# Batches 2 to 4 of an adapter and cross-attention kernel: ranks and logits by columns from standing weights and split x

## What is computed

```python
# first layer, on x
logits = einsum('bsh,nh->bsn', x, router_W) + router_b   # 8 experts
w = softmax(logits)
a_sum = einsum('bsh,arh->bsr', x, ctx)                   # 64 ranks, summed over the 4 context batches
y = einsum('bsr,nhr->bsnh', a_sum, lora_B)
out = nan_to_num(x + 0.5 * einsum('bsn,bsnh->bsh', w, y))
# second layer: cross-attention of out to ctx, 32 heads of 32, masked softmax,
# output projection, residual, layer norm with gain and shift
```

## Time and profile before

| what | value |
|---|---|
| median of 3 runs | 643.59 us (643.53 to 644.02) |
| the profiled execution | 643.8 us, its span 641.9 us |
| busy share PE / DVE / ACT / POOL | 98 / 78 / 53 / 42% |
| mean granted TensorE clock | 0.994 of full |
| DMA | 114.14 MB, 53.4% of the engines' time |

### The profile page before, as it was taken

One profiled execution on the slowest core, in us unless ns is written; L12 is line 12 of the kernel. 1 busy time (PEld: TensorE's weight loads), 2 busy tenths in 40 slices (PEclk: granted clock), 3 DMA queues, 4 the chain that ended last, 5 costly groups with the idle time before them and its releaser, 6 DMA issues.

```text
span 641.9 us, 10730 instructions
## 1 busy us (share of the span) xinstructions
PE 629.0 (98%) x3455; PEld 544.9 (85%) x3455; DVE 500.7 (78%) x907; ACT 337.7 (53%) x1000; POOL 268.0 (42%) x357
## 2 busy tenths in 40 slices
PE   8999999999999999999999999999999999999993
PEld 8988889888988889888888888888888888888883
DVE  5689995578457774677468899999999999999635
ACT  6454463123242242322268778787777787777520
POOL 0020001000020002000335556888888998888874
PEclk9999999999999999999999999999999999999997
DMA  8936685436774467722857993425354344522312
GB/s 299 410 128 177 178 306 179 156 82 210 233 264 149 114 235 240 280 80 68 258 151 261 383 376 96 132 99 181 82 165 150 117 148 120 174 85 84 114 50 99
DMA packets 103399, 114.14 MB, mean 178 GB/s; under 512 B 57008, under 2 KB 76080, under 8 KB 103344
## 3 DMA queue, kind: packets, MB, share of 16 engines
q1 hardware_dynamic: 103152, 113.20, 53.4%
q10 hardware_dynamic: 192, 0.26, 0.2%
HBM read 67.29 MB, written 46.14 MB: 177 GB/s over the span
## 4 chain that ended last, share of the span: by engine, by line
PE 95%; DVE 2%; DMA 1%; issue 1%; ACT 0%; DVEq 0%; SPq 0%; POOL 0%; POOLq 0%; ACTq 0%
PE ps L602 26%; PE ps L603 26%; PE ps L604 26%; PE ps L664 4%; PE ps L747 4%; PE ps L760 2%; PE ps L761 2%; PE ps L635 1%; PE ps L638 1%; PE ps L636 1%; PE ps L674 1%; DMA stage<-WkT 1%; DVE u_lo L885 0%; DVE cx_sum L981 0%; DVEq L209 0%
## 5 line engine op out<-in xcount | busy, mean ns | idle before, releaser
L1258 POOL TENSOR_TENSOR u_sb<-a_sb,w_sb 128x512 f32<-128x512 f32 x16 | 19.6, 1245 | 236.2 <-DVE w_sb L879 231.3
L602 PE MATMUL ps<-wo_hi,cx_hi 128*128 128x512 f32 (+1 forms) x264 | 105.9, 401 | 0.0
L1185 ACT ACTIVATE s_sb<-s_sb,s_min 128x64 f32<-128x64 f32 x256 | 85.8, 338 | 34.6 <-DVE s_min L959 34.6
L604 PE MATMUL ps<-wo_hi,cx_lo 128*128 128x512 f32 (+1 forms) x264 | 101.7, 385 | 0.0
L603 PE MATMUL ps<-wo_lo,cx_hi 128*128 128x512 f32 (+1 forms) x264 | 101.6, 385 | 0.0
L602 PE MATMUL ps<-act_hi,w_hi 128*128 128x512 f32 x256 | 100.9, 394 | 0.3 <-DVE q_sb L933 0.3
L603 PE MATMUL ps<-act_lo,w_hi 128*128 128x512 f32 x256 | 99.8, 390 | 0.0
L604 PE MATMUL ps<-act_hi,w_lo 128*128 128x512 f32 x256 | 99.8, 390 | 0.0
L1150 ACT ACTIVATE act_hi<-h_t 128x512 fp32r<-128x512 f32 x32 | 20.3, 633 | 111.8 <-DVE h_t L922 111.8
L981 DVE SCALAR_TENSOR_TENSOR cx_sum<-ps,bias_c,cx_raw 64x256 f32<-64x256 f32 x128 | 61.8, 483 | 8.8 <-ACT cx_raw L1199 4.8
L1269 POOL TENSOR_TENSOR s_sb<-s_sb,s_inv 128x512 f32<-128x512 f32 x64 | 67.0, 1047 | 0.0
(11 more groups left out here) (119 smaller groups left out, 1543.1 us busy)
## 6 DMA issues: line engine op xcount, KB each, us to landing
q_cols<-q_sb SPq DMA_DIRECT2D x32, 512.0 KB, 3.6
qb<-q_cols SPq DMA_DIRECT2D x64, 256.0 KB, 4.0
x_sb<-xT SPq DMA_DIRECT2D x32, 256.0 KB, 3.2
h_rows<-hn_sb SPq DMA_DIRECT2D x64, 128.0 KB, 3.0
output_weights<-wo_sb SPq DMA_DIRECT2D x32, 256.0 KB, 2.5
z_sb<-h_rows SPq DMA_DIRECT2D x16, 512.0 KB, 4.7
out<-z_sb SPq DMA_DIRECT2D x15, 512.0 KB, 2.9
stage<-WvT SPq DMA_DIRECT2D x8, 512.0 KB, 4.6
```

Source lines behind the costliest of these rows:

```text
L602: pe.matmul(dst, lh, rh, start=(first and j == 0), stop=False)
L604: mm = pe.matmul(dst, ll, rh, start=False, stop=(last and j == n - 1))
L1185: act.activation(s_sb[c % 4][:, h, :], s_sb[c % 4][:, h, :], ACT.Exp, bias=s_min[c % 2][:, h:h + 1], scale=-1.0, accum_out=s_sum[c % 2][:, ...
```

## The change

Batch 1 keeps its routing. For the other three:

- **Ranks by columns** (`tokens` on PE, `x_parts` on the others). x is split like every other operand: ACT copies x_hi, POOL (even chunks) or DVE (odd) subtracts x_lo, in three buffers. The adapter's weights stand: two stationary 128-column tiles per chunk, a_w[0] and a_w[1], made once by POOL in a new stage `adapter`; three matmuls of 512 columns per chunk give ps_a, with 64 ranks and 8 logits in rows. The low part of the adapter for ranks is placed in the columns that would be free, and DVE adds the two.
- **Softmax and spread** (`spread`, `weigh`): ACT copies ps_a to a_t, DVE transposes 32x32 blocks so that the logits of a token lie in one partition, does the softmax there (Exp on ACT), splits the weights into high and low, writes them in four blocks and transposes back; ACT copies w_rows.
- **Growing u** (`grow`): four matmuls with `choose` (ones in chosen rows, made once on POOL) as stationary operand spread two experts' weights each over 128 rows; DVE multiplies each by a_t (u_f), ACT copies u_hi, DVE subtracts u_lo. The pass over POOL and the transposes on PE are gone.
- **Places in the list**: chunks are split from the first query step on, used after the second, third and fourth (a step later each for batch 2); the spread behind the fourth, `weigh` behind the sixth, `grow` behind the seventh. For batch 2 one step later, and `grow` stands behind the first half's `leave`. Of the keys, parts 2 and 3 go behind the fifth and sixth step, k_hi of parts 2 and 3 share the buffers of 0 and 1 and wait for stores, the mask's load goes behind the first step. x's loads count on four semaphores, not one.

The core of the diff:

```diff
+            beside[i][0] += parts(i + 1, 0, 1, 2)
+            beside[i][1] += tokens(i + 1, 0, 1, 2) + parts(i + 1, 3, 4, 5)
+            beside[i][2] += tokens(i + 1, 3, 4, 5) + parts(i + 1, 6, 7)
+            beside[i][3] += tokens(i + 1, 6, 7) + [("spread", i + 1)]
+            beside[i][5] += [("weigh", i + 1)]
+            beside[i][6] += [("grow", i + 1)]
-            beside[i][3] += [("route", i + 1)]
-            beside[i][5] += [("expand", i + 1, 0)]
-            beside[i][6] += [("expand", i + 1, 1)]
...
+            def tokens(i, k):                                    # PE
...
+                pe.wait_ge(xlo_even if low_on_pool(k) else xlo_odd, n + 1)
+                pe.matmul(ps_a, a_w[0][:, k, :], x_h, start=(k == 0), stop=False)
+                pe.matmul(ps_a, a_w[0][:, k, :], x_l, start=False, stop=False)
+                pe.matmul(ps_a, a_w[1][:, k, :], x_h, start=False, stop=(k == KC - 1)).then_inc(a_mm, 1)
+            def grow(i):                                         # PE
...
+                pe.wait_ge(route_act, 3 * i + 1)
+                pe.wait_ge(t_ready, KC * i)
+                for j in range(RC):
+                    rows = slice(B * j, B * j + 4)
+                    pe.matmul(ps_w[j], choose[rows, :], w_rows[rows, :], start=True, stop=True).then_inc(w_mm, 1)
...
+            def x_parts(i, k):                                   # ACT
+                act.wait_ge(x_in[k // 2], 32 * (i + 1))
+                act.wait_ge(up_mm, KC * i)
+                if k >= 3:
+                    act.wait_ge(a_mm, KC * (i - 1) + k - 2)
+                act.activation(x_hi[k % 3][:], x_sb[:, k, :], ACT.Copy).then_inc(xhi_done, 1)
...
             def key_parts(b):                                    # ACT
                 if b == 0:
                     act.wait_ge(k_copied, KC)
-                if b == NB - 1:
-                    act.wait_ge(mask_step, 4)
+                if b >= 2:
+                    act.wait_ge(k_stored, 32 * b)
...
+            def grow(i):                                         # DVE
+                def low(j):
+                    dve.wait_ge(uhi_done, RC * i + j + 1)
+                    dve.tensor_tensor(u_lo[:, j, :], u_f[j % 2][:], u_hi[:, j, :], ALU.subtract).then_inc(ulo_done, 1)
+                for j in range(RC):
+                    if j >= 2:
+                        low(j - 2)
+                        dve.wait_ge(ulo_done, RC * i + j - 1)
+                    dve.wait_ge(w_mm, RC * (i - 1) + (j + 1 if j < 2 else RC))
+                    dve.tensor_tensor(u_f[j % 2][:], ps_w[j], a_t[:], ALU.mult).then_inc(u_made, 1)
+                low(2)
+                low(3)
```

246 lines of the change are left out of this document (179 added, 67 removed).

## The result

| | before | after |
|---|---|---|
| median (lowest to highest) | 643.79 us (643.53 to 644.02), 4 runs | 686.77 us (686.08 to 688.07), 4 runs |
| ratio, 95% interval | | 1.0668 [1.0654, 1.0681] |
| profiled execution, its span | 643.8, 641.9 | 686.1, 684.3 |

The direction and the chains that PE waits for held; the size did not, the clock's above all.

The account below looks back on a forecast made before the run. PE's in-order matmul stream was taken as the bound. Batches 2, 3 and 4 (+10.0, +8.3, +7.8, saved columns included) and the clock (+4) gave +30 on 643.8, less 0.2 for the median: 674 us, range 660 to 684.

Parts of the forecast that it names:

- Columns: PE's matmul work in batches 2 to 4: fewer columns streamed, -2.5 us per batch, -7.6 us in all.
- a) First x chunk: Before each batch's first token matmul, PE waits for x_hi behind act_hi, then POOL: 5.3, 3.7, 3.2 us.
- Rival 3: All waits are covered and only columns count, if x_hi leaves ACT before PE arrives: 636 us, chance 0.06.
- b) The spread: DVE's dependent chain after the last token matmul takes 5.5 us, bounds 4.5 and 9.
- rival 2: The spread is long, its links taking up to 0.6 us: +3.5 us per batch, 684 us, chance 0.13.
- c) Batch 2's keys: Late key stores and shared k_hi buffers stall PE 3.3 us at the weights, 4.0 us at the next query step.
- d) Split 5: Batches 3 and 4: output-weight split 5's load, released by split 3 behind the spread, delays u_f; 7.5 us stall each.
- e) The clock: PE's granted clock falls in two stalls surely, perhaps half the others: 4 us in all, bounds 0 and 18.
- f) Start: POOL's new work before 25 us may slow DVE's splits there: taken as nothing, bound +1.5 us.
- Rival 1: The output-weight load of split 5 is in time or the spread short, query stalls 3.6 us: 664 us, chance 0.17.

Follow-up runs that it names:

- e10_order: The change reordered only: batches 3 and 4 with later tokens and first update, output-weight splits before the spread, grow behind exits; batch 2 also reordered; 657.1 us.
- e4: The change with key part 2 split ahead of batch 2's spread instead of behind it, nothing else; 684.4 us.
- e6: The change with batches 3 and 4's new work one query step earlier, plus batch 2's x splits and key parts 2 and 3 earlier; 668.3 us.
- e1: The change with the output-weight split of query step 3 put ahead of the spread, nothing else; 677.3 us.
- e12_gaps: The kernel before, with idle gaps made by hand on PE ahead of second-half query step 4 in batches 1 to 3; 655.5 us.
- e13: e10_order with x splits 3 to 5 directly behind the first tokens, and weigh, grow and last output-weight split later in batches 3 and 4; 666.1 us.
- e7: The e1 kernel with grow of batches 3 and 4 moved behind the first half's exits; 678.7 us.

## Why the prediction was too low

Against the profiled execution it said +30, and +42.3 came.

- **Columns** (-7.6): the balance closes with this term within a microsecond (rest 11.2 against 10.6 us counted at the slow pitch; 5.2 against 5.2 in e10_order). Its part on the four weights' matmuls was wrong: that 4 rows would "neither cost nor save" fails, since the four run together, and my estimate of the saving is now 8.4 (7.6 and 0.8).
- **a) First x chunk**: 5.3, 3.7, 3.2 forecast; 5.20, 3.56, 3.06 measured. Right, in size too, though the later chunks were called in time and one was late by 0.53. (Rival 3 mixes starts and ends of x_hi: by its ends ACT stands 3.9, 2.3 and 1.8 us behind.)
- **b) The spread**: 5.5 forecast; in batch 3 from DVE's first link at 195.60 to its last at 200.86 plus 0.71, 6.0. Inside the bounds; rival 2 (+3.5 per batch) fell.
- **c) Batch 2's keys**: 3.3 and 4.0 forecast, 2.96 and 6.01 measured. The mechanism is shown by e4 and e6. The failed part is "2.8 us to land" for the last store: it was issued at 121.32 and ACT released at 125.81, 4.5 us, while part 2's took 2.3. The 2.8 is a median of four, and the last of the four, the one on this path, took 4.0 in the kernel before (DMA issues, 101.6 to 101.9 us):

```profile
keys<-k_lo SPq DMA_DIRECT2D x1, 256.0 KB, 4.0
```

Why the last one takes longer is open. The weights' matmuls, 0.5 us instead of 0.9, made the rest of the second stall.
- **d) Split 5**: 7.5 twice forecast; 8.54 and 8.90 measured. Shown by e1. In batch 3 the spread took 0.5 us more than taken, and from the start of split 3 (201.50) to ACT's split 5 (206.96) it was 5.5, the value of the earlier trace rows, not the 5.0 chosen. From u_f (208.23) to PE (215.06) it was 6.8, for 6.9 forecast. The miss is 2.4 over both batches.
- **e) The clock**: **the step that failed, in its size.** The prediction let two stalls surely bring a fall "and of the others perhaps half", four to five falls, and gave each a price of at most 2.6 us; yet it took 4 us for all, 0.9 per fall, and no step of it leads there. Measured 11.2. Matmuls ran at the slow pitch behind five of the seven stalls (not behind the last at the tokens; at the weights the clock fell while PE was already waiting again): five stretches of 7 to 12 matmuls in one piece, 1.4 to 2.4 us lost in each, and shorter pieces beside them. So the number of falls was about right, and the price in the sum was less than half of the measured one; 4.5 times 2.6 is 11.7. The Trainium skill, "TensorE: Matmul & The Clock Gate", section "HAM oscillation — how this bites in real kernels", has the cost paid anew behind each wait. Taken at its word, seven times 2.6 make 18, the upper bound; the trace lies between. The range left that bound out: 674 with 18 in place of 4 is 688, past its end of 684. (At its lower end, 674 less 4 and twice 0.5 is 669, not 667.) That 2.6 fits the 2.8 of e12_gaps is in part luck: it came from the slow first matmuls, where the granted clock reads 1.00. Window of the kernel before:

```profile
1.40:4.80 3.40, 3.36 (x8) 2.38 (x9) 0.56 (x1) 1.54 (x3) 0.09 (x1) 1.00 0.65 214
```

- **f) Start**: the first update's x_sb pass on DVE starts at 44.02 against 43.96 before. Nothing, as taken.

So 4.3 of the 12.3 us missing are stalls (c 1.7, d 2.4, the small one 0.5, less 0.4 in a), 7.2 the clock, and the 0.8 left is rounding in my steps: stalls of 34.5 less 7.6 and plus 4 are 30.9, not 30.1. Rival 1 did not occur, rival 3 neither, and e10_order says how far it is: with all waits moved as well as I could, 14.9 us remain, twice the 7.6 that the columns are worth. No version tried beats the kernel before; whether one could is open.

## What to carry to other kernels

Where one engine runs 98% busy, ask of each new wait on it not only how long it is but also whether the clock falls in it, and carry the number of falls times the price of one (here some 2 us) into the sum. Here most stalls of 3 us and more paid it, and some of 1.9 to 2.6 us in e6_keys_early and e10_order; and idle time in few long pieces cost more than in many short ones (e13 against e10). A dependent chain moved beside such an engine needs its loads and stores checked as well: a split behind the chain also delays the load that the split releases, and a stall cured alone often comes back in the next queue (e7, e13). Before writing such a change, compare what it saves per batch (2.5 us here) with the waits that even a good order leaves (4 to 6).

## What was not expected of the hardware

- A gap of 1.0 us left the granted clock at 1.00; one of 7.0 was followed by 5.5 us at 0.50; one of 3.1 left it at 1.00 in the profiled execution, while the stall of 3.6 in the changed kernel was followed by a fall (0.59 from 183 to 187). The stall of 3.1 ahead of batch 4's first tokens was followed by none in the changed kernel (1.00 from 269 to 276) and by one in e1_weights_first (0.58 from 266 to 270), at the same length. In e6_keys_early one of 1.88 was followed by a fall (0.51 from 252.8 to 255.8), in e10_order one of 2.20 by none (1.00 from 92.8 to 95.8).
- The fall came about a microsecond after PE had resumed there: the first matmul at 182.19 still took 0.47 us, the slow pitch starts at 183.0.
- Useless matmuls in the stalls gave back 8.5 us, with the waits as long in sum as before.
- Four matmuls on 4 rows each, in four groups of rows, lasted 0.50 us together, as long as the query matmul behind them alone (0.50 at 203.46).
- A DVE instruction with a single SBUF input (bound) took 1.51 us beside POOL's passes and 0.42 without; a cast of 32x128 took 1.20 beside POOL and 0.23 without.
